# The experts' biases by one-hot products on TensorE, epsilon on GpSimd, the skip term by a diagonal product, and a new task order

## The reference, cut to what matters

```python
delta = softplus(x @ Wd + bd);  Bm = x @ WB + bB;  Cm = x @ WC + bC;  A = -exp(A_log)
# for each token t, with 16 states for each of 128 features:
h = clip(exp(min(d_t * A, 2)) * h + clip(d_t * B_t, -2, 2) * x_t, -100, 100)
y = sum(h * C_t, states) + x_t * D_param                  # the skip term
routing = softmax(y @ Wr + br); e = argmax(routing); w = max(routing)
hid = silu(y @ up_w[e] + up_b[e])                         # 128 -> 512
out = y + w * (hid @ down_w[e] + down_b[e])               # 512 -> 128
a = norm(out) * ln_w + ln_b
x1 = layernorm(x + a)
x2 = layernorm(x1 + (silu(x1 @ wg) * (x1 @ wu)) @ wdn)    # 128 -> 384 -> 128, int weights / 127
```

## Time and profile before

| | |
|---|---|
| median of 3 runs | 1034.03 us (1033.85 to 1037.81) |
| the profiled execution | 1039.55 us, span 1037.4 us |
| busy in the span | PE 704.3 us, DVE 732.9 us, POOL 593.9 us, ACT 576.2 us |
| mean granted TensorE clock | 0.793 of full speed |
| start of `flag` (L934), chunks 0, 1, 2, 3 | 32.0, 101.7, 200.1, 311.1 us |
| the same, chunk 7 | 752.8 us |
| last state scanned | about 863.9 us |

### The profile page before, as it was taken

One profiled execution on the slowest core, in us unless ns is written; L12 is line 12 of the kernel. 1 busy time (PEld: TensorE's weight loads), 2 busy tenths in 40 slices (PEclk: granted clock), 3 DMA queues, 4 the chain that ended last, 5 costly groups with the idle time before them and its releaser, 6 DMA issues.

```text
span 1037.4 us, 14202 instructions
## 1 busy us (share of the span) xinstructions
PE 704.3 (68%) x4320; PEld 547.1 (53%) x4320; DVE 732.9 (71%) x1334; ACT 576.2 (56%) x1060; POOL 593.9 (57%) x468
## 2 busy tenths in 40 slices
PE   2445748864997388937995699649974896278144
PEld 1233527642875267726773487427762675167133
DVE  2799886589878987899788987898789853211031
ACT  6560637493767476656768476937562663235122
POOL 1365475268836794578637873679367835430440
PEclk8665858885999589966997599859985898579666
DMA  3433456734574447543674456445734482126100
GB/s 90 141 125 103 125 183 207 217 112 150 181 245 138 163 137 229 196 151 107 226 217 150 129 178 221 139 150 171 254 116 163 140 250 92 56 82 189 38 1 20
DMA packets 82061, 155.06 MB, mean 149 GB/s; under 512 B 9392, under 2 KB 51120, under 8 KB 81968
## 3 DMA queue, kind: packets, MB, share of 16 engines
q1 hardware_dynamic: 69168, 140.89, 42.3%
q0 software_dynamic: 4096, 8.40, 2.7%
q10 hardware_dynamic: 8704, 4.72, 1.7%
HBM read 138.56 MB, written 15.40 MB: 148 GB/s over the span
## 4 chain that ended last, share of the span: by engine, by line
PE 33%; DVE 18%; issue 14%; ACT 12%; POOL 12%; DMA 9%; SPq 1%; DVEq 0%; ACTq 0%; POOLq 0%
DVE state L1064 7%; PE psT L609 7%; PE psU L596 5%; PE psD L650 5%; DMA weights<-in_w_pack 4%; PE psY L490 3%; POOL prod L1091 3%; ACT decay L720 3%; DVE bst L1020 3%; PE psT L606 2%; DMA y_sorted<-rows_in 2%; PE psU L634 2%; POOL rows_in L1112 2%; PE psB L484 2%; POOL chosen_out L1120 2%
## 5 line engine op out<-in xcount | busy, mean ns | idle before, releaser
L1091 POOL TENSOR_TENSOR prod<-state,c_wide 128x1024 f32<-128x1024 f32 x128 | 301.2, 2358 | 229.8 <-DVE state L1064 218.0
L484 PE MATMUL psB<-parts,sel 128*128 128x512 bf16 x256 | 113.5, 462 | 170.1 <-DVE state L1064 168.6
L1055 DVE TENSOR_TENSOR psB<-dx,psB 128x512 f32<-128x512 f32 x256 | 168.1, 688 | 54.9 <-PE psB L484 48.3
L1064 DVE TENSOR_TENSOR_SCAN state<-decay,state,psB 128x512 f32<-128x512 f32 x128 | 163.8, 1280 | 14.0
L490 PE MATMUL psY<-ident,prod 128*128 128x128 f32 x1024 | 162.4, 315 | 8.1 <-POOL prod L1091 8.1
L490 PEld LDWEIGHTS psY<-ident,prod 128*128 128x128 f32 x1024 | 145.5, 166 | 21.4 <-POOL prod L1091 11.1
L1064 DVE TENSOR_TENSOR_SCAN state<-decay,psB 128x512 f32<-128x512 f32 x128 | 155.2, 1213 | 1.9 <-ACT decay L720 1.9
L720 ACT ACTIVATE decay<-delta,a_sb 128x1024 f32<-128x1024 f32 x128 | 139.7, 1140 | 28.0 <-DVE state L1064 25.8
L484 PEld LDWEIGHTS psB<-parts,sel 128*128 128x128 bf16 x256 | 26.6, 104 | 217.8 <-DVE state L1064 215.9
L759 ACT ACTIVATE hid<-psU,weights 128x128 f32<-128x128 f32 x352 | 100.4, 369 | 69.0 <-PE psU L596 67.0
L596 PE MATMUL psU<-yT_sorted,weights 128*128 128x128 f32 x704 | 98.9, 287 | 9.4 <-DMA weights<-in_w_pack 5.9
(11 more groups left out here) (138 smaller groups left out, 1181.8 us busy)
## 6 DMA issues: line engine op xcount, KB each, us to landing
c_wide<-c_rows SPq DMA_DIRECT2D x128, 512.0 KB, 4.6
weights<-in_w_pack SPq DMA_DIRECT2D x88, 578.0 KB, 4.5
xT_sb<-in_xT SPq DMA_DIRECT2D x8, 512.0 KB, 3.9
y_sorted<-rows_in SPq DMA_DIRECT2D x16, 256.0 KB, 5.1
xt<-in_x SPq DMA_DIRECT2D x8, 512.0 KB, 5.3
rows_out<-result SPq DMA_DIRECT2D x16, 256.0 KB, 5.6
out<-x ACTq DMA_DIRECT2D x16, 256.0 KB, 4.1
y_sorted<-rows_in SPq DMA_DIRECT2D x8, 192.0 KB, 5.9
```

The lines of the kernel that those rows point to most:

```text
L484: pe.matmul(tokens(psB, c, h), sel[:, s, :], parts[:, c.n % 2, h * HALF:h * HALF + c.hw], start=True, stop=True).then_inc(b_ready, 1)
L1055: v.tensor_tensor(tokens(psB, c, h), dx[:, n % 2, h * HALF:h * HALF + c.hw], tokens(psB, c, h), ALU.mult).then_inc(inp_ready, 1)
L1064: v.tensor_tensor_scan(state[:, g % NSTATE, t0:t0 + c.hw], decay[:, g % NDECAY, t0:t0 + c.hw], tokens(psB, c, h), before, ALU.mult, ALU.ad ...
L1091: g_.tensor_tensor(prod[:, g % NPROD, w], state[:, g % NSTATE, w], c_wide[:, g % NC, w], ALU.mult).then_inc(prod_ready, 1)
```

## The change

1. **Up bias.** `w_pack` loses its bias columns (512 KB for a block instead of 578 KB). The biases of all experts come once, at the start, and DVE splits them into three bf16 parts in `bias3` (96 partitions: rows 0, 32 and 64 on; `split_bias`). DVE forms, in `slots`, a one-hot column for each block, `of_block`. In `up`, behind each of the four fp32 products, PE adds a bf16 product of 96 rows by 128 columns that brings in the bias. ACT's `silu` is then a single instruction of 512 columns without a bias.
2. **Down bias.** The product of the row of ones with the bias row becomes a bf16 product of `of_block` and `bias3`.
3. **Skip term.** ACT no longer forms `xD`; PE multiplies each 128-token tile of x by the diagonal matrix `diag` in fp32, without transpose mode.
4. **FFN residual.** The two products with `ident127` become one fp32 product with `attn`. `affine` of the next chunk waits until `ff_down` has read `attn`.
5. **Epsilon.** L1028 leaves DVE; POOL adds epsilon in `rstd`, before the power, which now waits for it.
6. **Slots.** The scan of the block counts becomes two additions (`pairs`, `first_block`); a sum `expert_f` and a comparison `of_block` are added.
7. **Task order.** All five lists are written anew.

```diff
-W_DOWN, W_UPB, W_DOWNB = F, 2 * F, 2 * F + NF
+W_DOWN = F
 PE_ORDER = [
-    (0, "spread", 1, 0), (0, "spread", 1, 1), (-1, "yT_turn"), (1, "z"), (-1, "logits"), (0, "skip"),
...
-    (-1, "up", 10), (-1, "down", 9), (0, "add", 12), (1, "spread", 0, 0), (1, "spread", 0, 1), (-1, "down", 10),
-    (0, "add", 13), (0, "add", 14), (0, "add", 15),
+    (0, "spread", 2, 0), (-1, "yT_turn"), (0, "spread", 2, 1), (0, "skip"), (-1, "logits"), (0, "add", 0),
+    (0, "spread", 3, 0), (0, "spread", 3, 1), (0, "add", 1), (0, "spread", 4, 0), (0, "spread", 4, 1), (1, "bc"),
...
+    (-1, "up", 9), (-2, "ff_down", 1), (-1, "down", 8), (-1, "up", 10), (1, "spread", 0, 0), (1, "spread", 0, 1),
+    (-1, "down", 9), (0, "add", 13), (-1, "down", 10), (0, "add", 14), (0, "add", 15), (1, "spread", 1, 0),
+    (1, "spread", 1, 1), (2, "z"),
...
 DVE_ORDER = [
...
-    (-2, "ff_mul", 1, 2), (0, "scan", 14), (-1, "router_pick"), (-2, "stats", 1, 2), (1, "flag"), (0, "scan", 15),
-    (1, "scan", 0), (1, "scan", 1), (0, "router_shift"), (1, "scan", 2), (1, "scan", 3), (1, "scan", 4), (0, "slots"),
-    (-1, "combine", 0), (-1, "stats", 0, 0), (1, "scan", 5), (1, "scan", 6), (-1, "stats", 0, 1), (1, "scan", 7),
-    (2, "delta"), (1, "scan", 8), (-1, "combine", 1), (-1, "stats", 1, 0),
+    (-2, "ff_mul", 1, 1), (1, "flag"), (-2, "ff_mul", 1, 2), (0, "scan", 15), (-2, "stats", 1, 2), (1, "scan", 0),
+    (-1, "router_pick"), (1, "scan", 1), (1, "scan", 2), (0, "router_shift"), (1, "scan", 3), (1, "scan", 4),
+    (-1, "combine", 0), (-1, "stats", 0, 0), (1, "scan", 5), (0, "slots"), (1, "scan", 6), (-1, "stats", 0, 1),
+    (1, "scan", 7), (2, "delta"), (-1, "combine", 1), (1, "scan", 8), (-1, "stats", 1, 0),
...
 SP_ORDER = [
-    (-1, "c", 6), (-1, "c", 7), (-1, "c", 8), (-1, "c", 9), (-2, "rows"), (-1, "c", 10), (-1, "c", 11),
...
-    (-1, "weights", 2),
+    (-1, "c", 8), (-1, "c", 9), (-2, "rows"), (-1, "c", 10), (-1, "c", 11), (-2, "weights", 3), (-1, "c", 12),
...
+    (0, "c", 4), (0, "c", 5), (-1, "weights", 0), (-1, "weights", 1), (-1, "weights", 2), (0, "c", 6), (0, "c", 7),
...
             def add_skip(c):
-                pe.wait_ge(xD_ready, c.n + 1)
-                add_turned(c, -1, xD, True, False, skip_summed)
+                pe.wait_ge(xT_in, 16 * (c.n + 1))
+                for j in range(c.tiles):
+                    mm = pe.matmul(psY[:, j, :], xT_sb[:, c.n % 2, j * ROWS:(j + 1) * ROWS], diag[:, :],
+                                   start=(j % NJ == 0), stop=False, skip_group_check=True)
+                mm.then_inc(skip_summed, 1)
...
                     fill(u, c, task)
+                    pe.wait_ge(blocks_ready, 2 * n + 2)
                     for f in range(NF):
-                        mm = pe.matmul(bank[u][:, f * ROWS:(f + 1) * ROWS], weights[:, q % NW, f * 128:(f + 1) * 128],
-                                       yT_sorted[:, k * ROWS:(k + 1) * ROWS], start=True, stop=True)
+                        cols = slice(f * ROWS, (f + 1) * ROWS)
+                        pe.matmul(bank[u][:, cols], weights[:, q % NW, f * 128:(f + 1) * 128],
+                                  yT_sorted[:, k * ROWS:(k + 1) * ROWS], start=(f == 0), stop=False, skip_group_check=True)
+                        mm = pe.matmul(bank[u][:, cols], bias3[:, f * 128:(f + 1) * 128],
+                                       of_block[:, n % 2, k:k + 1].to_broadcast([96, ROWS]), start=False,
+                                       stop=(f == NF - 1), skip_group_check=True)
...
-                    pe.matmul(bank[d][:, 0:D], ones_row[:, :], weights[0:1, q % NW, W_DOWNB:W_DOWNB + D],
+                    pe.matmul(bank[d][:, 0:D], of_block[:, n % 2, k:k + 1].to_broadcast([96, ROWS]), bias3[:, F:F + D],
                               start=True, stop=False)
...
-                        pe.matmul(bank["D"][:, cols], x1h[:, cols], ident127[:, :], start=(j == 0), stop=False,
-                                  skip_group_check=True)
-                        pe.matmul(bank["D"][:, cols], x1l[:, cols], ident127[:, :], start=False, stop=False,
+                        pe.matmul(bank["D"][:, cols], ident127[:, :], attn[:, h * NJ + j, :], start=(j == 0), stop=False,
...
-                    for f in range(NF):
-                        ins = nc.scalar.activation(hid[:, k % 2, f, :], bank[u][:, f * ROWS:(f + 1) * ROWS], ACT.Silu,
-                                                   bias=weights[:, q % NW, W_UPB + f:W_UPB + f + 1])
-                    ins.then_inc(drained[u], 1)
+                    nc.scalar.activation(hid[:, k % 2, :, :], bank[u][:, :].rearrange("p (f r) -> p f r", f=NF), ACT.Silu
+                                         ).then_inc(drained[u], 1)
...
+            def split_bias():
+                src = y_sorted[:, 0:NF + 1, :].rearrange("p k d -> p (k d)")
+                part = [slice(32 * k, 32 * k + E) for k in range(3)]
+                v.tensor_copy(bias3[part[0], :], src[part[0], :])
+                v.tensor_copy(bias3[part[1], :], src[part[1], :])
+                v.tensor_copy(bias3[part[2], :], src[part[2], :]).then_inc(split_steps, 1)
+                dve.wait_ge(split_steps, 1)
+                v.tensor_tensor(src[part[1], :], src[part[1], :], bias3[part[1], :], ALU.subtract)
+                v.tensor_tensor(src[part[2], :], src[part[2], :], bias3[part[2], :], ALU.subtract
+                                ).then_inc(split_steps, 1)
...
-                    v.tensor_tensor_scan(first_block[:, 1:1 + E], ones_e[:, :], n_blocks[:, :], 0.0, ALU.mult, ALU.add
-                                         ).then_inc(slot_steps, 1)
+                    v.tensor_tensor(pairs[:, 2:2 + E], n_blocks[:, 1:1 + E], n_blocks[:, 0:E], ALU.add
+                                    ).then_inc(slot_steps, 1)
+                    dve.wait_ge(slot_steps, 7 * n + 3)
+                    v.tensor_tensor(first_block[:, 1:1 + E], pairs[:, 2:2 + E], pairs[:, 0:E], ALU.add
+                                    ).then_inc(slot_steps, 1)
...
+                    v.tensor_tensor(of_block[:, n % 2, 0:c.blocks], expert_f[0:96, 0:c.blocks],
+                                    row_expert.to_broadcast([96, c.blocks]), ALU.is_equal).then_inc(blocks_ready, 1)
...
                     ins.then_inc(stats_steps[h], 1)
-                    dve.wait_ge(stats_steps[h], 6 * turn + 2 * k + 1)
-                    v.tensor_scalar(ve[:, h, 0:c.hj], mv[:, h, 0:c.hj, 1], EPS if k < 2 else EPS * 127.0 * 127.0, None,
-                                    ALU.add).then_inc(stats_steps[h], 1)
...
+                    g_.tensor_tensor(ve[:, h, hj], mv[:, h, hj, 1], eps[:, int(k == 2), hj], ALU.add
+                                     ).then_inc(rstd_steps, 1)
                     g_.tensor_tensor(minus_mean[:, h, hj], mv[:, h, hj, 0], minus_one[:, hj], ALU.mult
                                      ).then_inc(rstd_steps, 1)
+                    pool.wait_ge(rstd_steps, 2)
                     g_.tensor_tensor(rstd[:, h, hj], ve[:, h, hj], minus_half[:, hj], ALU.pow).then_inc(rstd_steps, 1)
...
+                    before = [p for p in CHUNKS[:n] if p.halves > h]
+                    if before:
+                        pool.wait_ge(filled["D"], fills("D", before[-1], ("ff_down", h)))
```

More of the change, by code:

```diff
@@ L74 @@
[L74 to L78, removed]
@@ new lines @@
+    (0, "spread", 10, 0), (0, "spread", 10, 1), (-1, "up", 1), (-1, "down", 0), (-1, "sort_turn", 1), (-1, "up", 2),
+    (-1, "down", 1), (0, "spread", 11, 0), (-1, "sort_turn", 2), (0, "spread", 11, 1), (0, "add", 8), (-1, "down", 2),
+    (-2, "ff_down", 0), (-1, "up", 3), (1, "b_spread", 0), (0, "spread", 12, 0), (0, "add", 9), (0, "spread", 12, 1),
+    (-1, "up", 4), (-1, "down", 3), (-1, "up", 5), (-1, "down", 4), (-2, "x_turn", 1), (0, "spread", 13, 0),
+    (0, "add", 10), (0, "spread", 13, 1), (-1, "down", 5), (-2, "x_rest", 1), (-1, "up", 6), (1, "b_spread", 1),
@@ L100 @@
+    (-1, "silu", 5), (-2, "x_high", 1), (-1, "result", 5), (-2, "x_low", 1), (-1, "silu", 6), (-2, "gate", 1, 0),
+    (-2, "gate", 1, 1), (-1, "result", 6), (-1, "silu", 7), (-2, "gate", 1, 2), (-1, "result", 7), (-1, "silu", 8),
 ]
 DVE_ORDER = [
-    (1, "b_max"), (-2, "ff_mul", 0, 0), (-2, "ff_mul", 0, 1), (0, "scan", 9), (-2, "ff_mul", 0, 2), (0, "scan", 10),
-    (-2, "stats", 1, 1), (1, "bc_low"), (-2, "stats", 0, 2), (0, "scan", 11), (1, "bound", 0), (0, "scan", 12),
-    (0, "scan", 13), (1, "bound", 1), (1, "over"), (-2, "ff_mul", 1, 0), (-2, "ff_mul", 1, 1), (1, "dx"),
@@ L115 @@
[L115 to L118 removed]
+    (-3, "rstd", 1, 1), (-1, "prod", 11), (-3, "rstd", 0, 2), (-1, "prod", 12), (-1, "prod", 13), (-1, "prod", 14),
+    (-1, "prod", 15), (-3, "rstd", 1, 2), (-2, "gather", 0), (0, "prod", 0), (0, "prod", 1), (-2, "gather", 1),
@@ new lines @@
+    (-2, "gather", 2), (-2, "gather", 3), (-2, "gather", 4), (-2, "gather", 5), (-2, "gather", 6), (-2, "gather", 7),
```

(7 more changed lines are left out.)

146 lines of the change are left out of this document (78 added, 68 removed).

## The result

The changed kernel takes 1051.31 us (median of 4 runs, 1045.73 to 1053.36). The kernel before, on the same chips, takes 1034.73 us. The ratio is 1.0146, with a 95% interval of 1.0098 to 1.0195. So it is slower by 16.6 us, where 50 us less was forecast, and 1051 lies outside the range of 948 to 1020. The profiled execution took 1049.29 us (span 1047.5, mean granted clock 0.806).

A forecast was written before the change was run, and what follows sets the result against it. DVE and PE were taken to pace each other, DVE with the larger part. Six periods -48, light periods +1, setup +0.6 and the end -4 made -50.4, so 1034 - 50 = 984 us, own range 965 to 998, wider 948 to 1020.

The forecast's parts named there:

- I take -8, nearer to it: Sum for a full period: 8 us less, giving 102.5 us, chosen between -4.8 by the chain and -9.6 by DVE's work.
- the ledger: DVE's account of a full period: 93.1 - 10.2 + 0.6 = 83.5 us of work and small gaps, a gain of 9.6.
- stay as they are: Condition on the gain of 9.6 us a period: DVE's waits, 13.1 us a period, do not change.
- the chain's -4.8: Gain of a full period along the old chain of waits, if the order were as before: -4.4 -0.5 -0.5 +0.6.
- the stall of 4.61 us: Longest `ve` stall of the period, said to lie outside the chain, since DVE waited 1.03 us for a spread behind it.
- stalls hidden anyway: Rival for the full periods: only the chain's 4.8 us a period are gained, 1003 us; chance 0.14.
- the port stall moves: Rival: DVE's `combine`, `slots` and `delta` collide with POOL's `prod`; two a period give 1012 us, three 1026; chance 0.13.
- up to a `prod`, 2.34 us: Price set for each collision of a DVE instruction with POOL's `prod`: at most 2.34 us.
- as much again: Bound on the new task order: it can gain at most the 13.1 us of DVE waits and lose as much.
- The rival of products that don't pipeline: Rival: PE's bf16 bias products between fp32 ones take up to 0.41 us each, giving 1082 us; chance 0.10.
- 3 us in the sum: In the two light periods, `split_bias` costs DVE nine instructions, 5.4 us, of which 3 are put on the path.
- six periods -48, rest -2.4: Split of the forecast gain: six full periods -48; otherwise light periods +1, setup memsets +0.6, stretch after the last scan -4.

The follow-up runs named there:

- e1_code_only: The changed kernel with all its code edits but the five task lists of the kernel before: 1022.58 us, ratio 0.9889 to the kernel before.
- e4_ve_reduce: The kernel before, with the epsilon addition kept on DVE but done as a reduction over variance and a stored epsilon: 1029.84 us, ratio 0.9966.
- e5_combine_reduce: The changed kernel with `combine` as a reduction reading `chosen_out` alone, without expert weight and y: 1019.87 us, ratio 0.9856 to the kernel before.
- e11_new_mended: The changed kernel with `slots` before `combine` 0, `rank` before `bc`, `gather` 0 behind `prod` 1, `rstd` before `prod` 4, `over` before `c` 0: 1022.41 us.

## Why the prediction was wrong

**The step that failed first** is in the sum: "I take -8, nearer to it", the ledger. The ledger itself came true (83.3 us of DVE work in `e1_code_only`, 83.5 forecast). That its waits "stay as they are" did not: 17.4 us became 25.8. Even the chain's -4.8 was too much; -1.3 was measured over the four periods. What came in were waits for the FFN's products (17.5 us in four periods, none before) and for the spreads (35.2 for 20.0). The sign was in the text: the stall of 4.61 us was named as one that isn't in the chain, and for the shorter ones the chain showed one path where others ended just beside it. The rival "stalls hidden anyway", given 0.14, was right in its mechanism. It was still too kind in size, since it priced the epsilon at 4.4 us a period by the chain, and epsilon alone gained about 4 us in the whole kernel.

**The second is "the port stall moves"**, which had 0.13 as a rival and is what happened. In the changed kernel it broke the ledger's other term: DVE is busy for 94.2 us of a period in place of 83.5, with 19.3 idle. Its place was right, `combine` behind `scan` 4 and the additions of `slots`. Its unit was wrong: "up to a `prod`, 2.34 us", while DVE stood behind three of them for about 5.1. The row of 4.61 us had shown two in one stall, and so was the evidence against the unit. I had not walked POOL's new list to see how many `prod` pile up behind the gathers. The rule of the Trainium skill, page "SBUF — State Buffer", section "Who interferes with whom", names both sides of it: a DVE instruction that reads two SBUF tensors contends with a GpSimd instruction that reads SBUF, and a reduction never does. The runs agree with both, 6.29 us for four `combine` and 0.160 to 0.164 us for all 48 reductions.

**The rest of the order** was bounded by "as much again" as 13.1 us of waits and then left out of the likeliest case. SP's moved tasks stood in the lists, and their price, 4 us by the ratios and 9.0 by the medians, was nowhere in the sum. The same holds for `rank`, late for `slots` once those stand first.

**What held.** The bf16 product costs 0.10 to 0.11 us in PE's queue (0.09), and 0.047 by the end of the kernel, 2.0 us for a chunk where the chain had 2.2 for a period, though only 0.9 in the four full ones; the down bias takes 0.05 in PE's queue in place of 0.41 (0.09), which no run measured by itself; `silu` takes 0.597 us for 512 columns (0.60); the new `ve` on POOL 0.20 us. The rival of products that don't pipeline fell. PE's busy time is unchanged, 704.5 us. The stretch behind the last scan gained 6.6 us (4), 10.0 with the old lists. What `split_bias` cost, 3 us in the sum, is not shown: chunk 2 starts at 202.1 us with all the code under the old lists, but at 200.1 before and 194.7 with epsilon on POOL, and these last two differ by more than the term, though they do the same work up to there.

**Size of the whole.** Forecast: six periods -48, rest -2.4. Measured with the old lists: -11.6 in the medians. The new lists then cost 28.7 us.

**Open:** which chain holds a period at 108 to 109 us once the long stalls of `ve` and `combine` are gone, and what each part of the code other than epsilon and the up bias gained.

## What to carry to other kernels

Price a stall by what ends behind it: if the engine's next input arrives at the same time anyway, taking out 53 us of stall gains 4, as here. Before moving a DVE instruction that reads two SBUF tensors (or one of the other forms that stalled here, such as the addition of a constant), walk GpSimd's queue at its new place and count the instructions that stand there back to back, since the price can be all of them together. The reductions of `e4_ve_reduce` and `e5_combine_reduce`, put where such instructions had stalled, did not stall once.

## What the runs showed of the hardware that was not expected

- DVE did not get through between GpSimd's queued instructions. Four `combine` took 6.29 us behind three `prod` in a row, and ended 0.95 us after the third.
- The operands need not be large for it. An addition of 4 columns took 2.12 us beside a `prod`, a comparison of 11 columns 1.06 us beside `affine`; a reduction over 4 columns took 0.161 us in 48 of 48 cases.
- GpSimd's scatters, which only issue transfers, did not have this effect. In the kernel before, the second `combine` of a period (475.33 us) took 1.11 us for its four while such scatters ran on POOL. Beside gathers it is less clear: in `e11_new_mended` `of_block`, 0.17 us at least, began 0.3 to 0.6 us before a `prod`, while the last gather ran, and ended only with the `prod`.
- A small transfer, `over_row`, took 3.7 us to land with SP's old list (median; greatest 5.4) and 6.8 (8.0) with the new one. Putting it ahead of one 512 KB broadcast left it at 6.1 (8.0).
